# Layer 2: the product h·A for a batch is made one batch ahead, in group 3, in another PSUM bank, and its result is held twice

## The reference

```python
residual = hidden_states
x = _rmsnorm(hidden_states, ln1_w)
attn = _attention(x, Wq, Wk, Wv, Wo)          # 16 heads of 32, causal
mod = MOD_SCALE * jnp.tanh(attn @ A)          # A: 512 x 16
h = _rmsnorm(residual, ln2_w)
gate_pre = h @ W_in_base.T + mod * (h @ A) @ B
gate = jax.nn.silu(gate_pre)
up = h @ W_up_base.T
mlp_out = gate * up @ W_down.T
return residual + mlp_out
```

## Time and profile before

| | us |
|---|---|
| median of 3 runs (2812.46 to 2814.78) | 2813.64 |
| the profiled execution, its own time | 2813.49 |
| span of its trace, first to last instruction | 2811.7 |
| PE (TensorE) busy | 2643.1, 94% |
| DVE busy | 1585.5, 56% |
| ACT busy | 1333.8, 47% |
| POOL busy | 637.2, 23% |
| mean granted clock of TensorE | 0.975 |

### The profile page before, as it was taken

The page is one execution under the profiler, slowest core; times in us unless marked ns, Lnnn a source line. Parts: engine busy times, 40 slices in busy tenths (PEclk is TensorE's granted clock), DMA queues, the critical chain, the costliest instruction groups (busy, mean ns, idle before and its releaser), DMA issues.

```text
span 2811.7 us, 40923 instructions
## 1 busy us (share of the span) xinstructions
PE 2643.1 (94%) x13584; PEld 2021.7 (72%) x13584; DVE 1585.5 (56%) x4318; ACT 1333.8 (47%) x2755; POOL 637.2 (23%) x519
## 2 busy tenths in 40 slices
PE   6999999999768999999999889999999999999998
PEld 5777777777546666667667647888888888888886
DVE  5777777787735787787787775222222423333333
ACT  3777777777724666666666665111111321111111
POOL 3565566566220222222222111000000000000000
PEclk8999999999869999999999989999999999999999
DMA  6566656655534555555555544111111311111100
GB/s 147 116 140 138 146 133 145 147 141 137 137 102 106 126 117 115 127 117 117 131 116 118 133 82 166 47 47 46 48 46 46 103 58 47 47 46 46 46 30 30
DMA packets 173819, 276.44 MB, mean 98 GB/s; under 512 B 29125, under 2 KB 53445, under 8 KB 172997
## 3 DMA queue, kind: packets, MB, share of 16 engines
q1 hardware_dynamic: 170692, 260.57, 38.4%
q0 software_dynamic: 2304, 12.58, 1.3%
q10 hardware_dynamic: 640, 1.05, 0.1%
HBM read 97.03 MB, written 42.99 MB: 50 GB/s over the span
## 4 chain that ended last, share of the span: by engine, by line
PE 54%; DVE 7%; SPq 3%; ACT 3%; issue 3%; DMA 2%; POOL 0%; ACTq 0%; DVEq 0%; POOLq 0%
PE b_lin_ps L2455 13%; PE b_scores_ps L2466 13%; PE b_pv_ps L2436 6%; PE b_scores_t_ps L2436 6%; PE b_lin_ps L1985 5%; PE b_pv_ps L307 2%; DVE b_prob L290 2%; PE b_lin_ps L1948 2%; PE b_scores_t_ps L271 2%; DVE b_junk L202 1%; PE b_scores_ps L188 1%; SPq L258 1%; SPq L254 1%; PE b_lin_ps L2461 1%; DMA b_k_stack<-b_k_split 1%
## 5 line engine op out<-in xcount | busy, mean ns | idle before, releaser
L290 DVE TENSOR_TENSOR a_prob<-a_scores_t_ps,a_prob 128x384 fp32r<-128x384 f32 (+1 forms) x384 | 225.5, 594 | 140.1 <-ACT a_scores_t_ps L283 138.6
L282 ACT ACTIVATE b_prob<-b_scores_t_ps 128x384 fp32r<-128x384 f32 (+1 forms) x384 | 199.8, 520 | 211.9 <-PE b_scores_t_ps L273 191.1
L290 DVE TENSOR_TENSOR b_prob<-b_scores_t_ps,b_prob 128x384 fp32r<-128x384 f32 (+1 forms) x384 | 226.9, 594 | 120.9 <-ACT b_scores_t_ps L283 120.1
L282 ACT ACTIVATE a_prob<-a_scores_t_ps 128x384 fp32r<-128x384 f32 (+1 forms) x384 | 202.0, 526 | 161.0 <-PE a_scores_t_ps L273 135.4
L307 PE MATMUL a_pv_ps<-a_prob,a_value 128*65 128x512 f32 (+3 forms) x1024 | 272.6, 334 | 0.8 <-DVE a_prob L290 0.8
L307 PE MATMUL b_pv_ps<-b_prob,b_value 128*33 128x512 f32 (+3 forms) x1024 | 273.0, 335 | 0.1
L202 DVE CUSTOM_DVE_ANT_0 b_junk<-b_scores_ps,spare 128x512 bf16<-128x512 f32 (+3 forms) x512 | 226.9, 483 | 61.0 <-PE b_scores_ps L188 59.7
L202 DVE CUSTOM_DVE_ANT_0 a_junk<-a_scores_ps,spare 128x512 bf16<-128x512 f32 (+3 forms) x512 | 227.0, 484 | 28.0 <-PE a_scores_ps L188 25.8
L2399 DVE TENSOR_TENSOR b_res<-b_scores_ps,b_first_gate 128x512 f32<-128x512 f32 x64 | 44.3, 692 | 333.6 <-PE b_scores_ps L2466 333.6
L2399 DVE TENSOR_TENSOR stage<-b_scores_ps,b_junk 128x512 f32<-128x512 f32 x64 | 44.3, 692 | 329.1 <-PE b_scores_ps L2466 329.1
L1015 PE MATMUL a_lin_ps<-x_split,w_split 128*128 128x512 f32 x768 | 217.4, 399 | 4.0 <-DVE w_split L853 3.6
(11 more groups left out here) (303 smaller groups left out, 5874.8 us busy)
## 6 DMA issues: line engine op xcount, KB each, us to landing
a_q_stack<-a_q_split SPq DMA_DIRECT2D x192, 128.0 KB, 3.4
a_k_stack<-a_k_split SPq DMA_DIRECT2D x192, 128.0 KB, 3.6
b_q_stack<-b_q_split SPq DMA_DIRECT2D x192, 128.0 KB, 3.2
b_k_stack<-b_k_split SPq DMA_DIRECT2D x192, 128.0 KB, 3.6
spare<-h_t SPq DMA_DIRECT2D x16, 1024.0 KB, 6.2
stage<-in_x_t SPq DMA_DIRECT2D x8, 1024.0 KB, 6.5
a_sum_hi<-a_pv_raw SPq DMA_DIRECT2D x32, 256.0 KB, 3.8
spare<-a_pv_raw SPq DMA_DIRECT2D x32, 256.0 KB, 4.1
```

What stands on the lines that cost most here:

```text
L282: act.activation(at.prob_hi[:, k % at.ring, 0:w], at.scores_t_ps[:, k % 2, 0:w], ACT.Exp, scale=SCALE)
L290: dve.tensor_tensor(at.prob_lo[:, k % at.ring, 0:w], at.scores_t_ps[:, k % 2, 0:w], at.prob_hi[:, k % at.ring, 0:w], ALU.subtract).then_in ...
```

## The change

- `h_times_a` for batches 1 to 7 is made in group 3, slots 10 and 11, of the preceding batch, in bank 0 of `b_scores_ps`. It waits for ACT's copy of the row maxima of that group (`shift_copied`). Batch 0's stays in its group 1, in bank 1.
- ACT's copy of the result stands in group 0, slot 0, of its own batch (batch 0: in group 2, slot 0, as before), and PE waits for it in group 0, slot 1, ahead of the products of that slot (batch 0: group 2, slot 2, as before).
- The result has two places, used in turn: the old one in `b_late` for odd batches and 16 rows of the fourth tile of `spare` for even ones. ACT's copy therefore waits for the z term of the batch before the last one rather than of the last.
- SP waits for the seventh z term before it loads the MLP's first h into `spare`, in group 3 of the last batch.

```diff
--- before.py
+++ after.py
@@ -1148,6 +1148,10 @@
             yield from range(n * half + share(half, OUT_COUNT[n], at).start, n * half + share(half, OUT_COUNT[n], at).stop)
 
 
+def h_low_bank(b):
+    return 0 if b else 1
+
+
 def gate_value_items(b, g, slot):
 
     for bank, start in enumerate(VALUE_SLOTS):
@@ -1227,7 +1231,7 @@
         inv_root = sb("inv_root", [P, 2, TT])
         newton = sb("newton", [P, 2, TT])
         late = sb("late", [P, TT, SEQ])
-        (sum_hi, sum_lo, out_sum), h_low = [late[0:GH * RANK, i, :] for i in range(3)], late[0:RANK, 3, :]
+        (sum_hi, sum_lo, out_sum), h_low = [late[0:GH * RANK, i, :] for i in range(3)], [both.spare[0:RANK, 3, :], late[0:RANK, 3, :]]
         sums = sb("sums", [GH * TT, P])
         inverse = sb("inverse", [GH * TT, P])
         mod = at.shift_row[:, :].bitcast(F32)
@@ -1375,6 +1379,7 @@
                     mlp.load_z(sp, mlp.start, 0)
                 if last and g == 3:
                     sp.wait_ge(at.score_read, BATCH * GROUPS * UNITS)
+                    sp.wait_ge(z_made, BATCH - 1)
                     mlp.load_h(sp, mlp.start, 0)
                 if not first:
                     gather(*group(b, g, -1))
@@ -1607,8 +1612,8 @@
 
             def h_times_a(b):
                 act.wait_ge(h_low_made, b + 1)
-                at_least(act, z_made, b)
-                act.activation(h_low[:, :], at.scores_ps[0:RANK, 1, :], ACT.Copy).then_inc(h_low_copied, 1)
+                at_least(act, z_made, b - 1)
+                act.activation(h_low[b % 2], at.scores_ps[0:RANK, h_low_bank(b), :], ACT.Copy).then_inc(h_low_copied, 1)
 
             def step(b, g):
                 last = is_last(b)
@@ -1646,7 +1651,7 @@
                             tanh(b - 1)
                         if slot == 4:
                             z_part(b - 1)
-                    if g == 2 and slot == 0:
+                    if slot == 0 and (g == 2 if zero else g == 0):
                         h_times_a(b)
                     if last and g == 1 and 5 <= slot < 6 + KC:
                         act.wait_ge(o_made, BATCH * TT)
@@ -1793,7 +1798,7 @@
             def z_term(b):
                 dve.wait_ge(mod_done, b + 1)
                 dve.wait_ge(h_low_copied, b + 1)
-                dve.scalar_tensor_tensor(out=mod[:, :], in0=mod[:, :], scalar=MOD_SCALE, in1=h_low[:, :],
+                dve.scalar_tensor_tensor(out=mod[:, :], in0=mod[:, :], scalar=MOD_SCALE, in1=h_low[b % 2],
                                          op0=ALU.mult, op1=ALU.mult).then_inc(z_made, 1)
 
             def z_part(b):
@@ -2002,10 +2007,12 @@
 
             def h_times_a(b, items):
                 for x in items:
-                    if x == 0:
-                        pe.wait_ge(at.score_read, (b * GROUPS + 3) * UNITS)
+                    if x == 0 and b:
+                        pe.wait_ge(at.shift_copied, b * GROUPS + 1)
+                    elif x == 0:
+                        pe.wait_ge(at.score_read, 3 * UNITS)
                     c, (w, a) = x // 3, PASSES[x % 3]
-                    mm = pe.matmul(at.scores_ps[0:RANK, 1, :], low_a_split[:, w, c, :], h_split[:, a, c, :],
+                    mm = pe.matmul(at.scores_ps[0:RANK, h_low_bank(b), :], low_a_split[:, w, c, :], h_split[:, a, c, :],
                                    start=(x == 0), stop=(x == 3 * KC - 1))
                     if x == 3 * KC - 1:
                         mm.then_inc(h_low_made, 1)
@@ -2027,7 +2034,9 @@
                         pe.wait_ge(low_ready, b + 2)
                     if slot == 2 and g == 1 and not zero:
                         pe.wait_ge(mod_done, b)
-                    if slot == 2 and g == 2:
+                    if slot == 2 and g == 2 and zero:
+                        pe.wait_ge(h_low_copied, 1)
+                    if slot == 1 and g == 0 and not zero:
                         pe.wait_ge(h_low_copied, b + 1)
                     if slot >= 2:
                         pv_unit(pe, at, b, g, slot - 2, slice(0, -1))
@@ -2044,8 +2053,11 @@
                         modulation(b - 1)
                     if g < 2 and not last:
                         project_out(b + 1, out_items(g, slot))
-                    if g == 1 and slot in (10, 11):
-                        h_times_a(b, share(3 * KC, 2, slot - 10))
+                    if slot in (10, 11):
+                        if g == 1 and zero:
+                            h_times_a(0, share(3 * KC, 2, slot - 10))
+                        if g == 3 and not last:
+                            h_times_a(b + 1, share(3 * KC, 2, slot - 10))
                     if g == 2 and 1 <= slot < 5 and not last:
                         turn_h(b + 1, slot - 1)
                     if g == 3 and slot in (8, 9) and has(b, 2):
```

## The result

The changed kernel takes 2838.3 us (median of 4 runs, 2835.5 to 2850.5) against 2814.2 for the kernel before. The ratio is 1.0095, with a 95% interval of 1.0081 to 1.0109: slower by some 24 us, clear of the 0.2% that can be told. The profiled execution took 2836.96 us and its span is 23.4 us longer than that of before.

A forecast was written before the change was run, and what follows sets the result against it. Layer 2's attention alternates between saturated TensorE and a chain of waits over DVE and ACT; 2813.5 + 23.4 (borders) + 7.2 (clock, batches 1 to 6) + 0 (batch 7) = 2844.1 us, range 2826 to 2859.

The forecast's parts named there:

- What is removed is hidden: Group 1, batches 1 to 6: removing 2.80 us of matmuls a batch only lengthens TensorE's waits, the first by about 1.4.
- The addition and the new wait: Borders, group 3 to group 0: matmuls +2.80, cover −0.52, wait for ACT's copy +1.30, so 3.58 us a batch.
- Border 6: Border of batch 6 to 7: a stack's DMA wait takes part of the delay; 1.9 us slower (bounds 1 and 3.1).
- The clock: Near group 2's start, batches 1 to 6: fall to 1.2 GHz, +1.2 us a batch in place of −0.7; 7.2 together.
- The gain of 0.7 us from ACT's copy: Groups 1 to 2, batches 1 to 6: ACT loses the copy and starts unit 1 earlier, 0.7 us less a batch.
- Batch 7: Last batch: removed matmuls gain up to 2.5 us, but the lower clock eats it; 0 (bounds −2.5 and +1.5).
- a lower clock at the borders too: Rival: waits at the seven borders bring half clock, 1.7 us each on top, 2856 us; chance 0.18.
- The case without a lower clock: Rival: borders as forecast, clock stays up behind group 1, 6.7 us gained, 2830.2 us; chance 0.14.
- The partly absorbed delay: Rival: ACT's copy comes earlier or its wait hides behind DVE; a border costs 2.3 us, kernel 2823; chance 0.07.
- The faster one: Rival: at the border of group 3 and group 0 a later unmoved wait swallows the delay, 2807 us; chance 0.05.

The follow-up runs named there:

- experiment 2: Kernel before with only 1 of the product's 12 matmuls in each of batches 1 to 7, nothing added: 2815.9 us, ratio 1.0010.
- experiment 5: Kernel before with 12 unread matmuls added in group 3, slots 10 and 11, of batches 0 to 6: 2825.9 us, ratio 1.0053.
- experiment 3: Changed kernel with the old 12 matmuls made again, unread, in group 1, slots 10 and 11, of batches 1 to 7: 2832.2 us, ratio 1.0062.
- experiment 6: Changed kernel with ACT's copy ahead of unit 0's exponentials and the 12 unread matmuls in group 1: 2826.1 us, ratio 1.0053.
- experiment 7: Kernel before with the product one slot earlier (group 1, slots 9 and 10) and ACT's copy in group 1, slot 11: 2816.9 us, ratio 1.0024.

## Why the prediction was right

I gave 2844.0 us, 2826 to 2859, slower with 0.94; it is 2838.3. Step by step:

- **What is removed is hidden.** Right. The first wait grew by 1.39 us where I said about 1.4, and experiment 2 shows that taking out 77 of the matmuls gains nothing.
- **The addition and the new wait.** Right in kind, and a border costs 3.36 us on the mean where I had 3.58 (3.5, if the border is compared with the 23.47 us of experiment 2, since one border of before happened to be 0.8 us longer than the rest). The idle time at line 307 is 1.45 us where I had 1.3, with the releaser that I named. But the split inside the sum was wrong. I took the 12 matmuls at 2.80 less 0.52 of cover, 2.3, and the wait at 1.3. By itself the addition costs 2.5 (experiment 5) and the wait's share is 1.0 (26.99 less 25.99). I had missed that a late unit 0 opens a wait of its own in slot 2, of 0.7 us, behind which a part of the new wait hides. Mending the copy's place therefore gained 0.84 us a border and not 1.2. The term for the matmuls was too small and the one for the wait too large; that their sum is so close is in part luck.
- **Border 6.** 1.62 us where I had 1.9. Sum of the borders: 21.8 us where I had 23.4.
- **The clock.** Right: it falls once in each of batches 1 to 6 near the start of group 2, for 6.8 us, as long as I had taken from batch 7, and the stretch is 1.22 us longer where I had +1.2. That figure too hides two errors that cancel: +1.9 for the clock and −0.7 for the gain, where the runs show 1.6 and 0.4. It is now shown and not only argued: with the clock held by unread matmuls the same code takes 1.6 us less (experiment 3). The Trainium skill ("TensorE: Matmul & The Clock Gate", Part 1) says that idleness brings the throttle back. These traces agree in kind: 1.27 of 3.40 us busy was followed by 0.50, and the filled stretch, 2.71 of 3.40, by 1.00. As a rule for a single batch it isn't enough: in experiment 2 the same wait stands in six batches and the clock fell for 6.8 us in only two of them.
- **The gain of 0.7 us from ACT's copy.** The size is off: experiment 3 shows 0.4 us (20.04 against 20.43). No run has both the matmuls and the copy taken out with the clock at 1.00, so the 0.7 itself was not measured. I had let nearly the whole advance of unit 1's exponential through; that DVE, full behind it, passes on less is likely but not shown.
- **Batch 7.** I had 0 and it is −1.1 us. That this is the removal's doing isn't shown: experiments 3, 5 and 6, with all 12 matmuls in that place, have −0.94, −1.25 and −0.78 us.
- **The rest of the distance** to the forecast, 6 us by the median and 7 by the profiled execution, is the 3.8 us by which other places of layer 2's attention were shorter after than before, most of it where the clock had been low before, and the borders and batches 0 and 7 above.

Of the rivals, a lower clock at the borders too didn't come: the granted clock is 1.00 there in both profiles of the changed kernel. The case without a lower clock falls with the falls seen in six batches. The partly absorbed delay had 2.3 us a border, and it is 3.36. The faster one would have needed a wait that swallows the delay; there is none but in batch 7.

## What to carry to other kernels

Idle time of an engine in one stretch and saturation in another are worth looking up before a step is moved: here 2.8 us of matmuls a batch cost nothing where they stood and 2.5 us where they went. A consumer's wait for a copy has to be priced with what the copying engine does first in its own order. And work in the gaps of a busy TensorE can be holding its clock; before it is taken out of a stretch, look at what the clock did after stretches as empty as the one that it will leave.

## What the runs showed of the hardware that was not expected

- Matmuls that nobody reads made the kernel faster: 84 of them, 2838 to 2832 us, because TensorE stayed at 2.4 GHz at the start of group 2 (1.6 us a batch less in that stretch).
- In a stretch bound by ACT and DVE a low clock of 3.4 us was absorbed in experiment 2 (20.4 to 20.5 us against 20.3), though not plainly in experiment 7, and one of 6.8 us cost 1.6 us; in a saturated stretch 6.8 us at 0.50, with the stall of 1.8 us before it, cost 5.0 us.
